# A fused four-layer transformer on one core: first expert tile picked by 0/1 matmuls, expert results scattered to token order

## The reference

```
# layer 2 (here: stage l2f), 2048 tokens, hidden 1024
logits = xf @ wg.T + bg
vals, idx = top_k(logits, 2)            # weights = softmax over the two
out += silu(xf @ Wgate[e].T) * (xf @ Wup[e].T) @ Wdown[e].T * weights[:, e]
x = x + tanh(g_ffn[2]) * out
# layer 3, second half (stage l3f), 2048 tokens, hidden 1024
expert = argmax(xn @ gate_w + gate_b)   # xn = layernorm(x)
x = x + gelu(xn @ w1[expert]) @ w2[expert]
```

## Time and profile before

| | |
|---|---|
| Median of 3 runs | 3384.02 us (3381.76 to 3389.62) |
| The profiled execution | 3399.18 us, of which the span from first to last instruction is 3397.3 us |
| TensorE busy | 2913.8 us (86%), mean granted clock 0.936 |
| VectorE, ScalarE, GpSimd busy | 1648.4, 1292.7, 1264.3 us |
| Stage l2f | about 1706 to 2232 us of the span |
| Stage l3f | about 3130 to 3397 us |
| DMA moved | 169.97 MB |

### The profile page before, as it was taken

The page is one execution under the profiler, slowest core; times in us unless marked ns, Lnnn a source line. Parts: engine busy times, 40 slices in busy tenths (PEclk is TensorE's granted clock), DMA queues, the critical chain, the costliest instruction groups (busy, mean ns, idle before and its releaser), DMA issues. The chain is left out here.

```text
span 3397.3 us, 40621 instructions
## 1 busy us (share of the span) xinstructions
PE 2913.8 (86%) x15682; PEld 1553.7 (46%) x15693; DVE 1648.4 (49%) x3228; ACT 1292.7 (38%) x1784; POOL 1264.3 (37%) x986
## 2 busy tenths in 40 slices
PE   7888899999999999487949999838888899988596
PEld 3455334444344443233438898713333223223495
DVE  4635454554554644575631222246653776774101
ACT  4432444344334344365411111123443565564131
POOL 2341366565675667501251111224655210001212
PEclk9999899999999999798979999968998999999798
DMA  3100000000000000000034555410000000000364
GB/s 112 33 1 8 29 5 5 10 5 9 7 5 5 10 1 1 25 1 27 1 123 170 209 203 192 152 47 5 3 11 35 1 1 1 1 1 26 126 235 157
DMA packets 58946, 169.97 MB, mean 50 GB/s; under 512 B 8813, under 2 KB 36898, under 8 KB 45956
## 3 DMA queue, kind: packets, MB, share of 16 engines
q0 software_dynamic: 20128, 121.52, 9.8%
q1 hardware_dynamic: 38628, 45.85, 4.3%
HBM read 143.62 MB, written 23.72 MB: 49 GB/s over the span
## 5 line engine op out<-in xcount | busy, mean ns | idle before, releaser
L1501 POOL TENSOR_TENSOR l1x_added<-l1x_added,l1x_probs 128x1024 f32<-128x1024 f32 x224 | 527.3, 2354 | 264.9 <-ACT l1x_probs L1766 198.6
L1863 DVE TENSOR_REDUCE l1x_tops<-l1x_ring 128x1 f32<-128x512 f32 x512 | 326.6, 685 | 203.8 <-PE l1x_ring L1577 203.3
L1115 DVE TENSOR_REDUCE l3a_halves<-l3a_ring 128x1 f32<-128x512 f32 x512 | 324.7, 683 | 98.4 <-PE l3a_ring L960 94.1
L1766 ACT ACTIVATE l1x_probs<-l1x_slots 128x1024 f32<-128x1024 f32 x256 | 262.0, 1024 | 239.7 <-PE l1x_slots L1621 237.9
L1614 PE MATMUL l1x_slots<-l1x_Q,l1x_K 64*128 64x512 f32 x1152 | 311.2, 618 | 7.4 <-ACT l1x_probs L1764 4.8
L1076 ACT ACTIVATE l3a_probs<-l3a_slots 128x1024 f32<-128x1024 f32 x256 | 248.1, 1021 | 159.2 <-PE l3a_slots L980 159.2
L1636 PE MATMUL l1x_pv<-l1x_probs,l1x_V 128*64 128x512 f32 x1152 | 285.0, 611 | 0.0
L3350 DVE TENSOR_TENSOR l2f_hh<-l2f_sg,l2f_hid 128x256 f32<-128x256 f32 (+1 forms) x184 | 69.9, 381 | 244.1 <-ACT l2f_sg L3190 201.2
L980 PE MATMUL l3a_slots<-l3a_Q,l3a_K 32*128 32x512 f32 x1024 | 149.7, 634 | 35.4 <-ACT l3a_probs L1076 34.6
L3110 PE MATMUL l2f_hid<-l2f_xgT,l2f_gate 128*128 128x256 f32 (+1 forms) x736 | 167.8, 351 | 4.8 <-DVE l2f_hh L3350 3.3
L3190 ACT ACTIVATE l2f_sg<-l2f_hid 128x256 f32<-128x256 f32 (+1 forms) x184 | 64.5, 352 | 282.3 <-PE l2f_hid L3110 272.8
(11 more groups left out here) (691 smaller groups left out, 5060.3 us busy)
## 6 DMA issues: line engine op xcount, KB each, us to landing
l1x_w<-in_l_qkv SPq DMA_DIRECT2D x16, 384.0 KB, 2.9
slots_in<-zeros POOLq DMA_DIRECT2D x1, 4992.0 KB, 24.1
l2f_xg<-slots_in SPq DMA_DIRECT2D x16, 256.0 KB, 6.7
slots_out<-l2f_y SPq DMA_DIRECT2D x16, 256.0 KB, 3.1
x<-in_x SPq DMA_DIRECT2D x4, 512.0 KB, 13.9
l1f_w<-in_l_w SPq DMA_DIRECT2D x2, 1024.0 KB, 7.2
x<-x SPq DMA_DIRECT2D x4, 512.0 KB, 2.9
l3f_base<-x SPq DMA_DIRECT2D x1, 2048.0 KB, 8.4
```

The costliest lines, as they stand in the source:

```text
L1115: nc.vector.tensor_reduce(halves[:, k % 2, col:col + 1], bank_of(banks[e]), AX.X, ALU.max).then_inc(s["bank_done"], 1)
L1501: ins = nc.gpsimd.tensor_tensor(added[h][:], added[h][:], probs[:, n % PROBS, :, :], ALU.add)
L1766: ins = nc.scalar.activation(p, s2[m % 2], ACT.Exp)
L1863: ins = nc.vector.tensor_reduce(tops[:, e * NT + t, h:h + 1], bank, AX.X, ALU.max)
```

## The change

Four things change, in both expert stages and in the first stage:

- Rows of `slots_in` get 16 words more (ROW = 272 instead of 256), which hold the number of the token row (plus 2048 for the second choice), written by GpSimd. There is one such tensor for each value of `top`; both are cleared in stage l0x, and the 16 words of every row are set there to a spare row number, by copies from DRAM to DRAM.
- Tile 0's rows no longer come through DRAM. VectorE makes 16 matrices of 0 and 1 (`picks`, 128 tokens by 256 slots each) and TensorE multiplies `xn` by them (`pick`), with 16 `keep_busy` matmuls ahead. The keep-busy matmuls of chunks 2 and 3 go. The order of the tiles stays the same for both values of `top`, though it is computed in another way.
- GpSimd reads the row numbers that came with a tile (`take_ids`) and scatters each tile's results (`y`) to `rows_out` in token order, one indirect DMA per 128 rows. SyncE collects them at the end with four plain loads per choice. The gathers and SyncE's stores go.
- The second choice's scatter waits for the landing of the first's; in l3f tile 1's first weights are fetched in the middle of the scatter. The computation of `share` moves behind tile 0's result.

```diff
+ROW = D + 16
...
-    io["slots_in"] = nc.dram_tensor("slots_in", (slot_units(2) * P, D), F32, kind="Internal").ap()
-    io["slots_out"] = nc.dram_tensor("slots_out", (slot_units(2) * P, D), F32, kind="Internal").ap()
+    for top in (1, 2):
+        io[f"slots_in{top}"] = nc.dram_tensor(f"slots_in{top}", (slot_units(top) * P, ROW), F32, kind="Internal").ap()
+    io["rows_out"] = nc.dram_tensor("rows_out", (2 * TOK + slot_units(2) * P, D), F32, kind="Internal").ap()
...
-            if slots_out is not None:
-                pool.dma_start(slots_out.rearrange("(n p) d -> p n d", p=P),
-                               c.zeros[:].unsqueeze(1).broadcast_to([P, slots_out.shape[0] // P, D])).then_inc(c.cleared, 16)
+            for rows, spare in to_clear:
+                pool.dma_start(rows[:, 0:D].rearrange("(n p) d -> p n d", p=P),
+                               c.zeros[:].unsqueeze(1).broadcast_to([P, rows.shape[0] // P, D])).then_inc(c.cleared, 16)
+                pool.dma_start(rows[:, D:], spare).then_inc(c.cleared, 16)
...
+        row_no, slot_no = sb("row_no", [P, TT]), sb("slot_no", [P, pick_cols])
+        pick_to = sb("pick_to", [P, PICKED, ST, 16])
+        to_row = sb("to_row", [P, TILES, ST], U32)
+        picks = [yg[:, :, j, 0:tiles[j][1] * P] for j in range(PICKED)]
...
-            def store(v):
-                first, n = tiles[v]
-                sp.dma_start(tiles_of(slots_out, first * P, n), y[v % 2][:, 0:n, :]).then_inc(s[f"y_stored{v % 2}"], 16)
-
             sp.wait_ge(s["scattered0"], 16 * TT)
-            load(0)
             if top > 1:
                 sp.wait_ge(s["scattered1"], 16 * TT)
-            load(1)
-            for v in range(TILES):
-                if v + 2 < TILES:
-                    sp.wait_ge(s["turned"], v + 1)
-                    load(v + 2)
-                sp.wait_ge(s["y_ready"], v + 3)
-                store(v)
+            load(PICKED)
+            load(PICKED + 1)
+            for v in range(PICKED):
+                first, n = tiles[v]
+                sp.dma_start(pick_to[:, v, 0:n, :], tiles_of(slots_in, first * P, n)[:, :, D:]).then_inc(s["pick_to_loaded"], 16)
+            for v in range(PICKED, TILES - 2):
+                sp.wait_ge(s["turned"], v + 1)
+                sp.wait_ge(s["ids_taken"], v + 1)
+                load(v + 2)
+
+            def collect(j):
+                for n in range(NC):
+                    sp.dma_start(yg[:, n * CT:(n + 1) * CT, j, :], tiles_of(rows_out, j * TOK + n * CH, CT)).then_inc(gathered[j][n], 16)
+
+            for i in range(2):
+                sp.wait_ge(s[f"y_stored{i}"], 16 * sum(n for v, (_, n) in enumerate(tiles[:-1]) if v % 2 == i))
+            if top > 1:
+                collect(0)
+            sp.wait_ge(s["last_stored"], 16)
+            collect(top - 1)
...
+            pool.wait_ge(s["r_loaded"], n_cst)
+            pool.tensor_copy(xn[:, :, D:], row_no[:].unsqueeze(2).broadcast_to([P, TT, ROW - D])).then_inc(s["ids_set"], 1)
+
+            def scatter(j, t):
+                pool.indirect_dma_start(slots_in, bass.IndirectOffsetOnAxis(at_row[:, j, t:t + 1], 0), xn[:, t, :], None).then_inc(s[f"scattered{j}"], 16)
+
             pool.wait_ge(s["rows_ready"], 1)
             fetch_hid(0)
             fetch_down(0)
-            pool.wait_ge(c.cleared, 16)
+            pool.wait_ge(c.cleared, 64)
+            pool.wait_ge(s["ids_set"], 1)
             pool.wait_ge(s["slots_ready"], 1)
             for t in range(TT):
-                pool.indirect_dma_start(slots_in, bass.IndirectOffsetOnAxis(at_row[:, 0, t:t + 1], 0), xn[:, t, :], None).then_inc(s["scattered0"], 16)
-            fetch_hid(1)
+                if top == 1 and t == TT // 2:
+                    fetch_hid(1)
+                scatter(0, t)
+            if top > 1:
+                fetch_hid(1)
             fetch_down(1)
             if top > 1:
+                pool.wait_ge(s["scattered0"], 16 * TT)
+                pool.tensor_scalar(xn[:, :, D:], xn[:, :, D:], float(TOK), None, ALU.add).then_inc(s["ids_moved"], 1)
+                pool.wait_ge(s["ids_moved"], 1)
                 pool.wait_ge(s["slots_ready"], 2)
                 for t in range(TT):
-                    pool.indirect_dma_start(slots_in, bass.IndirectOffsetOnAxis(at_row[:, 1, t:t + 1], 0), xn[:, t, :], None).then_inc(s["scattered1"], 16)
-            for v in range(2, TILES):
-                pool.wait_ge(s["hid_ready"], (v - 1) * MH)
-                fetch_hid(v)
-                pool.wait_ge(s["down_done"], v - 1)
-                fetch_down(v)
-
...
+                    scatter(1, t)
+
+            def take_ids(v):
+                n = tiles[v][1]
+                if v < PICKED:
+                    pool.wait_ge(s["pick_to_loaded"], 16 * PICKED)
+                    ids = pick_to[:, v, 0:n, 0]
+                else:
+                    pool.wait_ge(s[f"xg_loaded{v % 2}"], 16 * ((v - PICKED) // 2 + 1))
+                    ids = xg[v % 2][:, 0:n, D]
+                pool.tensor_copy(to_row[:, v, 0:n], ids).then_inc(s["ids_taken"], 1)
+
+            for v in range(TILES):
+                if v >= PICKED:
+                    take_ids(v)
+                if v + 2 < TILES:
+                    pool.wait_ge(s["hid_ready"], (v + 1) * MH)
+                    fetch_hid(v + 2)
+                    pool.wait_ge(s["down_done"], v + 1)
+                    fetch_down(v + 2)
+                if v < PICKED:
+                    take_ids(v)
+                pool.wait_ge(s["ids_taken"], v + 1)
+                pool.wait_ge(s["y_ready"], v + 3)
+                for t in range(tiles[v][1]):
+                    pool.indirect_dma_start(rows_out, bass.IndirectOffsetOnAxis(to_row[:, v, t:t + 1], 0), y[v % 2][:, t, :],
+                                            None).then_inc(s["last_stored" if v == TILES - 1 else f"y_stored{v % 2}"], 16)
...
             def keep_busy(n):
                 for _ in range(n):
-                    nc.tensor.matmul(routed[:].rearrange("p a n -> p (a n)"), zero_w[:], zero_x[:], start=True, stop=True)
+                    nc.tensor.matmul(out_ps[1][:].rearrange("p a n -> p (a n)"), zero_w[:], zero_x[:], start=True, stop=True)
 
             pe.wait_ge(s["zeros_set"], 2)
             keep_busy(16)
             turn_chunk(0)
             for n in range(NC):
-                keep_busy(6)
+                if n < 2:
+                    keep_busy(6)
                 if n + 1 < NC:
                     turn_chunk(n + 1)
...
+            keep_busy(16)
+
+            def pick(v):
+                cols = tiles[v][1] * P
+                for k in range(KD):
+                    for t in range(TT):
+                        if k == 0:
+                            pe.wait_ge(s[f"picked{v}"], t + 1)
+                        last = nc.tensor.matmul(turn[:, k, 0:cols], xn[:, t, k * P:(k + 1) * P], picks[v][:, t, :],
+                                                start=t == 0, stop=t == TT - 1)
+                last.then_inc(s["turned"], 1)
+
             def turn_tile(v):
                 i = v % 2
-                pe.wait_ge(s[f"xg_loaded{i}"], 16 * (v // 2 + 1))
+                pe.wait_ge(s[f"xg_loaded{i}"], 16 * ((v - PICKED) // 2 + 1))
...
-            turn_tile(0)
+            pick(0)
             for v in range(TILES):
                 hidden(v)
-                if tiles[v][1] == 1:
+                if v + 1 == PICKED:
+                    for t in range(tiles[v][1]):
+                        down(v, t)
+                    turn_tile(v + 1)
+                elif tiles[v][1] == 1:
                     if v + 1 < TILES:
                         turn_tile(v + 1)
                     down(v, 0)
-                elif v == 0:
...
             nc.vector.tensor_copy(at_row[:, 0, :], at[:, 0, :]).then_inc(s["slots_ready"], 1)
+            for t in range(TT):
+                nc.vector.tensor_scalar(picks[0][:, t, :], slot_no[:, 0:SLOTS], at[:, 0, t:t + 1], None, ALU.is_equal).then_inc(s["picked0"], 1)
...
-                dve.wait_ge(s[f"y_stored{v % 2}"], 16 * (v // 2 + 1))
+                if v >= 2:
+                    dve.wait_ge(s[f"y_stored{v % 2}"], 16 * sum(size for u, (_, size) in enumerate(tiles[:v]) if u % 2 == v % 2))
                 nc.vector.tensor_copy(y[v % 2][:, 0:n, :], out_ps[v % 2][:, 0:n, :]).then_inc(s["y_ready"], 1)
+                if v == 0 and top > 1:
...
-                    dve.wait_ge(gathered[j][n], 16 * CT)
+                    dve.wait_ge(gathered[j][n], 16)
```

92 lines of the change are left out of this document (42 added, 50 removed).

## The result

The changed kernel takes 3338.3 us (median of 4 runs, 3330.5 to 3339.3) against 3384.0 (4 runs, 3381.8 to 3389.6) on the same chip: ratio 0.9858, 95% interval 0.9838 to 0.9877. The forecast was 3339. Its profiled execution took 3337.5 us, span 3335.8; that of before 3399.2, span 3397.3.

What follows compares the result with a forecast made beforehand. TensorE, 98 to 99% busy, bounds the long stretches, leaving the stages' heads and tails to gain. +5.5 - 3.1 - 19.8 - 16.8 - 10.5 = -44.7 us from 3384.0 gives 3339; 8 in 10 lie in 3320 to 3362.

Steps and rivals of the forecast that it cites:

- A: Start of the first stage: four DMAs issued by GpSimd instead of one clear delay the start, +5.5 us.
- C: Head of l2f: picked tile 0 ends by 1773, but tile 1 still waits for the second scatter; -3.1 us.
- D: Tail of l2f: one last scatter, four plain loads and the last adds replace the gathers; -19.8 us.
- E: Head of l3f: tile 0 picked, one scatter only, tile 1 starts near 3193.3 instead of 3211.57; -16.8 us.
- F: Tail of l3f: as in l2f, but VectorE's x*g + base holds the last scatter; -10.5 us.
- G: Steady stretches of tiles: GpSimd's added scatters and conversions per tile fit its slack; 0 us.
- Rival 3: First stage: queued clears hold GpSimd until 71 us instead of 10.28, +61, total 3395 us; chance 0.06.
- B: Keep-busy matmuls removed between chunks in both stages: routing starts 1.8 us earlier per stage, counted inside C and E.
- Rival 1: Head of l2f: the second scatter doesn't hold tile 1, 17 us more gained, 3322 us; chance 0.07.
- Rival 4: Both heads: VectorE's 16 picks block GpSimd's first scatters fully, 2 x 4.8 us more, 3349 us; chance 0.15.
- rival 2: Steady stretches: TensorE waits 0.5 us in each of 36 tiles, +18, 3357 us; chance 0.12.

Runs made afterwards that it cites:

- first pair: The first profiled executions of the kernel before (3399.2 us) and of the changed kernel (3337.5 us).
- second pair: A second trace of each kernel, both unedited: before profiled at 3381.7 us, changed at 3340.7 us.
- late_clears: Changed kernel with the four clearing DMAs issued behind GpSimd's scalings of units 4 to 7 of l0x; 3343.2 us, ratio 0.9860.
- picked2: Changed kernel with tile 1 of l2f also picked by 0/1 matmuls; 3354.1 us, ratio 0.9884.
- nopick: Changed kernel with tile 0 loaded through the DRAM rows again instead of picked; 3372.6 us, ratio 0.9949.
- early_base: Changed kernel with l3f's x * g + base computed in two halves behind tile 1's copy, not the last; 3345.9 us, ratio 0.9865.
- old_tail: Changed kernel with the earlier tail: plain stores in slot order and GpSimd's indirect gathers at the end; 3389.8 us, ratio 0.9997.
- before_again: The kernel before, unchanged, run again for a second trace; 3389.0 us, ratio 0.9997.
- after_again: The changed kernel, unchanged, run again for a second trace; 3348.6 us, ratio 0.9887.
- paused: Changed kernel with GpSimd waiting after every fourth scatter until these have landed, in both stages; 3360.0 us, ratio 0.9916.

## Why the prediction was right, and where not

The forecast time was hit, and partly by luck. The terms in us, for the two pairs of traces (the rest of the program adds -1.0 in the first pair, apart from the first stage's own variation, and -0.3 in the second):

| term | forecast | first pair | second pair |
|---|---|---|---|
| A start | +5.5 | +3.8 at the first matmul | +3.9, kept to l0f |
| C head of l2f | -3.1 | -3.0 | +4.1 |
| D tail of l2f | -19.8 | -19.6 | -21.0 |
| E head of l3f | -16.8 | -21.0 | -9.4 |
| F tail of l3f | -10.5 | -11.4 | -11.5 |
| G steady | 0 | -3.8 | -2.2 |
| gap behind l2f | none | -4.5 | -4.4 |

**A** was mis-sized: three further issues of 1.88, 1.53 and 1.31 us with no time between, 4.7 in all and not 6.5. Everything that was late at the start stayed late, and late_clears gives it back whole. Rival 3, a queue that holds GpSimd for 71 us, is refuted by the same rows.

**B** is small: from the first turn to the rank matmul 19.1 us became 18.6 in l2f, and 19.0 became 16.7 and 17.2 in l3f; 20.9 in late_clears, so this stretch varies as well.

**C and E** failed in their most general step: that tile 0, once picked, ends when its matmuls are summed up. That holds in the first trace, down to 1775.2 for the forecast 1773, 1795.74 for 1794.0 and a start at the lower clock. It doesn't hold in most others. Of the 9 traces with tile 0 picked and unbroken scatters in l2f, one (the first) was free of the stall, and picked2 met it later; the other 7 took 36 to 40 us from the first hidden matmul to down(0) instead of 13.9. In l3f one of 8 was free, and the others took 8.6 to 12.4 us instead of 7.0, behind a hand-over of 4.4 to 8.8 us instead of 1.1. The sign was in the trace of before: its own tile 0 of l2f took 21.2 us, with 3.29 us of TensorE idle, while the second scatter ran:

```profile
1785.55 1.03 PE L3110 MATMUL l2f_hid<-l2f_xgT,l2f_up 128*128 128x256 f32 x4
1789.86 1.30 PE L3110 MATMUL l2f_hid<-l2f_xgT,l2f_gate 128*128 128x256 f32 x4 [3.29 <-DVE l2f_hh L3350]
```

TensorE's third and fourth step there were 2.9 and 7.6 us late already. In nopick, where no scatter runs beside tile 0, it took 16.2 us from the same lower clock. The prediction has no word on this wait, and the change moves tile 0 right under the scatters. So E is about -10 in a usual execution (69.8 to 73.8 us to down(1), against 81.4 and 84.2) instead of -16.8, and C about +4 (104 to 109 against 99.8 and 103.9). Where nothing held it, as in the first trace, E came to -21.0, 4.2 past the forecast: the rows were asked for 1.4 us sooner after the turn than forecast, landed in 5.3 us instead of 6.4 to 6.7, and found TensorE warm, which the forecast had priced at 1.5. Rival 1 (tile 1 not held by the second scatter) is refuted: its load was issued at 1789.46, behind that scatter, and TensorE waited 20.54 us for the rows.

**D and F** came as worked out, to 1.2 us, by the loads' price at the rate of l3f_base: the last of the four lands 8.4 us (l2f) and 8.5 us (l3f) after the first is issued, where the forecast had 8.9 to 9. One part was not foreseen: the first lands after 3.9 to 4.0 us, and from there VectorE adds without a stop, 16 adds in 6.4 us, which end 0.3 us later than the last four alone would. In l2f the first choice's adds fill the time until then, all but 0.20 us (2193.30 to 2200.32 above), so there VectorE's 32 adds set the length of the tail as much as the loads do. The hold of the last scatter in F is confirmed by early_base (4.49 us to 0.98). The Trainium skill ("SBUF — State Buffer", SBUF: two separate sides) describes such a hold for a whole instruction of VectorE; the trace agrees for the one of 4.47 us.

**Rival 4**, the same hold by the 16 picks, is refuted: they took 4.8 us back to back, and GpSimd's issues beside them in l2f (two fetches and the first scatter) took 0.96, 0.93 and 1.02 us.

**G** is zero in the middle, as said, and rival 2 with it: from copy to copy the tiles of l2f take 21.16, 20.94 and 11.04 us in all four traces. What was missed lies at its end. Before, the last copy of l2f came 12.8 and 14.4 us after the one before it, now 10.6: the gathers of the first choice were issued beside the last tile. That the old tail is the cause is shown by old_tail (14.4 us again), and the semaphore's record shows that it is the hold described below: TensorE's last matmuls of l2f end at 2194.58 in before and its step comes at 2198.37, 3.8 us late, beside nine gathers issued back to back since 2187.61; 2.2 us late in before_again, 3.8 in old_tail, 0.01 in after. These are the 3.8 and 2.2 us by which the last copy came later than now. And 4.4 us behind the last add, which old_tail brings back: the next stage starts later when the old tail, with its indirect gathers, stands right before it. C and E lost 14.6 us against the forecast in the second pair. These two (6.6), D's and F's excess (2.2) and A (1.6) covered 10 of them: +3.9 + 4.1 - 21.0 - 9.4 - 11.5 - 2.2 - 4.4 = -40.5 for a forecast of -44.7, and by its ratio -38. In the first pair C and E lost nothing and the terms sum to -59.5 us, while the medians lie 45.6 us apart, since that execution of before lay 15 us above the median of its kernel. So the forecast hit the median with errors of both signs inside it.

So the gain is that of the tails: old_tail, with heads and picks as changed, is at 0.9997. The 10 us that the head of l3f wins in a usual execution go to the start (+3.9) and to the head of l2f (+4).

## What to carry to other kernels

A small transfer per tile, done while the next tile is computed, beats one sweep of indirect DMAs at the end: the sweep costs its own issue time (16 x 1.28 us here), holds up what is computed beside it (2 to 4 us at the last copy of l2f), and comes with a later start of the next stage (4 us). Work that is moved under a long burst of GpSimd's indirect DMAs should not be priced by its duration alone; look in the trace for what already runs under such a burst and whether its handovers come on time. And one trace a side wasn't enough here: the same head was 63 us in one execution and 72 in the next.

## What was not expected of the hardware

TensorE was held up in most executions while GpSimd issued indirect DMAs back to back (one per 1.28 us). The DMA engines are no busier with the stall than without: in 1750 to 1780 us their share is 0.54 in the second trace and 0.58 in the first, clean one. TensorE's semaphore steps came up to 24.6 us late in after_again and 25.5 in late_clears, and matmuls themselves stalled (picked2), until the burst was over; with a pause after every four it was gone in the one trace that has it. The gathers of the kernel before did the same to the last step of l2f, 2.2 to 3.8 us late in all three traces that have them there. Groups of one or two indirect DMAs per tile do nothing measurable: from copy to copy the tiles take the same time as before. The Trainium skill (the same page and section) says that TensorE's and ScalarE's SBUF ports never wait for anyone; the traces don't contradict that as a statement on ports, but whoever takes it to mean that they run undisturbed is off by 20 us here. What exactly is shared stays open: no run tells descriptors, semaphore steps of the landing DMAs and the transfers apart, nor why two executions of one kernel differ in it.

The traces' own records thin out with it. The 16 scatters of l3f step their semaphore 256 times as they land; the trace has all 256 steps in the clean first trace of after and 173 in paused, but only 33 to 39 in the seven held heads. Where TensorE has no tile to compute under the burst there are 213 to 231 (both traces of before, and nopick). In l2f it is the same for the second choice: 256 steps in after and in paused, 29 to 32 in the seven held heads, and 40 and 42 in the two traces of before, whose tile 0 is computed there. So the hold and the loss of records come together. Every trace is one of a profiled execution, and no run tells whether the recording has a part in the hold.

The first stage has a variation of its own, 6 to 7 us before l0f's first matmul in either kernel (158.2 or 165.4 before; 162 or 168 to 169 after), which no run explains.
